# Softmax layers: the order of exponentials, masks, probability splits, bias additions and normalisations on ScalarE and VectorE

## The reference

```
u     = h @ h.T / sqrt(384)                      # per graph, 64 x 64
a     = softmax(u)
delta = a * adjacency
attn  = delta / (sum(delta) + 1e-10)
hl, hs, hr = h @ wl.T + bl,  h @ ws.T + bs,  h @ wr.T + br
ctx   = (attn * upper) @ hl + diag(attn) * hs + (attn * lower) @ hr
o     = (ctx - mean(ctx)) / sqrt(var(ctx) + 1e-12) * g + beta
h     = relu(o)
```

## Time and profile before

| | |
|---|---|
| median of 3 runs | 1877.37 us (1875.14 to 1880.11) |
| the profiled execution | 1874.41 us, its span 1872.6 us |
| TensorE matmul busy | 1732.7 us, 93% of the span |
| VectorE busy | 1254.2 us, 67% |
| ScalarE busy | 886.8 us, 47% |
| GpSimd busy | 817.1 us, 44% |
| largest group | L1092, the values: 637.4 and 399.5 us of matmul time |
| the chain that ended last | TensorE 32% of the span, of it 23% on L1092; VectorE 10%, ScalarE 6% |

### The profile page before, as it was taken

How to read it: one execution, slowest core, us unless ns; L and a number is a source line. 1 busy time by engine, 2 the same in 40 slices (tenths; PEclk the granted TensorE clock), 3 DMA queues, 4 the chain that set the end, 5 groups by cost and what they waited for, 6 DMA issues and landing times.

```text
span 1872.6 us, 30639 instructions
## 1 busy us (share of the span) xinstructions
PE 1732.7 (93%) x9856; PEld 1639.1 (88%) x9856; DVE 1254.2 (67%) x2738; ACT 886.8 (47%) x1783; POOL 817.1 (44%) x848
## 2 busy tenths in 40 slices
PE   7999999999999999995999898999998989989894
PEld 6988888888989888885989898989898989989894
DVE  4586776868585876866567566566575666665656
ACT  4536454554546454554443535444445344343442
POOL 5242432334242432325455356364553564545624
PEclk9999999999999999997999999999999999999997
DMA  6004020301202020302200202002002020020100
GB/s 210 7 23 143 27 85 6 106 6 37 75 22 84 28 84 6 107 16 75 71 1 20 87 0 88 18 20 87 0 30 77 19 87 0 20 87 0 71 1 34
DMA packets 76373, 91.98 MB, mean 49 GB/s; under 512 B 29616, under 2 KB 67504, under 8 KB 76336
## 3 DMA queue, kind: packets, MB, share of 16 engines
q1 hardware_dynamic: 76336, 91.51, 14.8%
HBM read 53.75 MB, written 25.17 MB: 42 GB/s over the span
## 4 chain that ended last, share of the span: by engine, by line
PE 32%; DVE 10%; ACT 6%; issue 5%; DVEq 0%; POOL 0%; ACTq 0%; POOLq 0%
PE s_work L1092 23%; PE s_work L1104 4%; PE b_turn L1053 3%; DVE b_z L1433 2%; DVE b_z L1390 2%; ACT b_z L1191 2%; DVE s_prob_lo L1373 2%; DVE s_fstats L1439 1%; ACT b_z L1199 1%; PE b_score_ps L101 1%; DVE b_turn L1368 1%; ACT s_v_hi L1185 1%; ACT s_expo L1173 1%; DVE s_own L1378 1%; DVE s_v_own L1356 0%
## 5 line engine op out<-in xcount | busy, mean ns | idle before, releaser
L1092 PE MATMUL s_work<-b_w_hi,b_ht 128*128 128x384 f32 x2304 | 637.4, 351 | 0.0
L1092 PEld LDWEIGHTS s_work<-b_w_hi,b_ht 128*128 128x128 f32 x2304 | 440.9, 198 | 0.0
L1092 PE MATMUL s_work<-b_w_lo,b_ht 128*128 128x384 f32 x1152 | 399.5, 347 | 0.0
L359 PE MATMUL g_work<-b_ht,b_w_hi 128*128 128x512 f32 x1152 | 357.5, 391 | 9.8 <-DVE b_w_lo L678 9.8
L1260 POOL TENSOR_TENSOR s_v_lo<-s_v_full,s_v_hi 128x384 fp32r<-128x384 f32 x256 | 242.3, 959 | 266.3 <-ACT s_v_hi L1185 265.8
L612 POOL TENSOR_TENSOR g_qv_lo<-g_v_full,g_qv_hi 128x384 fp32r<-128x384 f32 x128 | 132.7, 1055 | 376.9 <-ACT g_qv_hi L496 376.9
L1356 DVE TENSOR_TENSOR s_v_full<-s_work,b_bias 128x384 f32<-128x384 f32 x256 | 141.1, 556 | 180.2 <-PE s_work L1092 180.2
L359 PEld LDWEIGHTS g_work<-b_ht,b_w_hi 128*128 128x128 f32 x1152 | 215.9, 188 | 52.0 <-issue 9.8
L1092 PEld LDWEIGHTS s_work<-b_w_lo,b_ht 128*128 128x128 f32 x1152 | 228.4, 198 | 0.0
L359 PE MATMUL g_work<-b_ht,b_w_lo 128*128 128x512 f32 x576 | 225.8, 392 | 0.0
L701 DVE TENSOR_TENSOR g_qv_lo<-g_work,g_qv_hi 128x512 fp32r<-128x512 f32 x192 | 128.8, 688 | 117.4 <-ACT g_qv_hi L484 115.6
(11 more groups left out here) (142 smaller groups left out, 3201.9 us busy)
## 6 DMA issues: line engine op xcount, KB each, us to landing
b_x_in<-in_x_t SPq DMA_DIRECT2D x16, 768.0 KB, 7.0
g_x_res<-in_x SPq DMA_DIRECT2D x16, 768.0 KB, 7.6
b_x_in<-x SPq DMA_DIRECT2D x16, 768.0 KB, 5.1
s_x_res<-b_x_in SPq DMA_DIRECT2D x16, 768.0 KB, 5.8
x<-b_z SPq DMA_DIRECT2D x15, 768.0 KB, 3.8
out<-b_z SPq DMA_DIRECT2D x15, 768.0 KB, 3.6
b_a_tr<-in_adj_t SPq DMA_DIRECT2D x64, 64.0 KB, 3.4
g_a_nat<-in_adj SPq DMA_DIRECT2D x32, 64.0 KB, 2.4
```

Source lines behind the costliest of these rows:

```text
L359: mm = pe.matmul(bank[:], w, h, start=(n == 0), stop=(n == len(pairs) - 1))
L1092: mm = pe.matmul(bank[:, 0:H], h, w, start=(n == 0), stop=(n == len(pairs) - 1))
```

## The change

On TensorE the exponentials of layer 1 are turned after value 2 instead of value 3. On ScalarE the probability copies of layer 0 go ahead of the value copies of tile 0 and of normalise; in layer 1 they stay behind both, but ahead of the value copies of tile 1, and normalise goes ahead of the value copies of tile 0. `final_normalise` goes from ahead of the next exponentials to behind normalise of the next unit (steps of unit 3 and, one pass later, unit 0). On VectorE the masks and splits go ahead of all bias additions but number 0 (layer 0) or numbers 0 to 2 or 3 (layer 1), maximum goes ahead of variances, and deviations goes ahead of bias 1 and 2.

```
@@ tensor, one_pass
-                    for j in range(4):
+                    for j in range(SIDES):
                         values(i, unit, j)
                     if layer_of(unit) == 1:
                         turn_exponentials(i, unit)
-                    for j in range(4, 7):
+                    for j in range(SIDES, 7):
                         values(i, unit, j)
@@ scalar
-            def first_half(i, unit):
-                exponentials(i, unit)
-                values_hi(i, unit, 0)
-
-            def second_half(i, unit, more):
+            def rest(i, unit, more):
                 values_hi(i, unit, 1)
-                probabilities_hi(i, unit)
                 if more:
                     turn_out(i, unit + 1, 0)
                     turn_out(i, unit + 1, 1)
...
-            def one_pass(i, last):
+            def one_pass(i, first, last):
 
                 for unit in range(UNITS):
                     more = not (last and unit == UNITS - 1)
                     if more:
-                        first_half(i, unit + 1)
-                    normalise(i, unit, more)
-                    if more:
-                        second_half(i, unit + 1, not (last and unit == UNITS - 2))
-                    if unit >= STREAMS:
-                        final_normalise(i, unit - STREAMS, tiles=NT if more else NT // 2)
+                        exponentials(i, unit + 1)
+                        if layer_of(unit + 1) == 0:
+                            probabilities_hi(i, unit + 1)
+                            values_hi(i, unit + 1, 0)
+                            normalise(i, unit, more)
+                        else:
+                            normalise(i, unit, more)
+                            values_hi(i, unit + 1, 0)
+                            probabilities_hi(i, unit + 1)
+                        if unit == 0 and not first:
+                            final_normalise(i - 1, 1)
+                        if unit == UNITS - 1:
+                            final_normalise(i, 0)
+                        rest(i, unit + 1, not (last and unit == UNITS - 2))
+                        if last and unit == UNITS - 2:
+                            final_normalise(i, 0)
+                    else:
+                        normalise(i, unit, more)
+                        final_normalise(i, 1, tiles=NT // 2)
...
-            first_half(0, 0)
+            exponentials(0, 0)
+            probabilities_hi(0, 0)
+            values_hi(0, 0, 0)
             for n in range(SIDES):
                 weight_hi(n)
-            second_half(0, 0, True)
...
+            rest(0, 0, True)
+            one_pass(0, True, False)
+            with act.Fori(1, PASSES - 1) as i:
+                one_pass(i, False, False)
+            one_pass(PASSES - 1, False, True)
@@ vector, up_to_contexts
-                for j in range(3, 6):
+                if layer_of(unit) == 1:
+                    probabilities(i, unit)
+                    biased_value(i, unit, 3)
+                    probabilities_lo(i, unit)
+                else:
+                    biased_value(i, unit, 3)
+                for j in range(4, 7):
                     biased_value(i, unit, j)
-                probabilities(i, unit)
-                biased_value(i, unit, 6)
-                probabilities_lo(i, unit)
@@ vector, one_pass
-                    variances(i, unit)
                     if not (last and unit == UNITS - 1):
                         if layer_of(unit + 1) == 1:
                             maximum(i, unit + 1)
-                        for j in range(SIDES):
+                            variances(i, unit)
+                            biased_value(i, unit + 1, 0)
+                        else:
+                            variances(i, unit)
+                            probabilities(i, unit + 1)
+                            biased_value(i, unit + 1, 0)
+                            probabilities_lo(i, unit + 1)
+                        deviations(i, unit)
+                        for j in range(1, SIDES):
                             biased_value(i, unit + 1, j)
-                        deviations(i, unit)
                         up_to_contexts(i, unit + 1, last, s if layer == 1 else None)
...
-            for j in range(SIDES):
+            probabilities(0, 0)
+            biased_value(0, 0, 0)
+            probabilities_lo(0, 0)
+            for j in range(1, SIDES):
                 biased_value(0, 0, j)
```

More of the change, by code:

```diff
@@ L1223, in one_pass @@
                     if more:
-                        first_half(i, unit + 1)
-                    normalise(i, unit, more)
-                    if more:
-                        second_half(i, unit + 1, not (last and unit == UNITS - 2))
-                    if unit >= STREAMS:
-                        final_normalise(i, unit - STREAMS, tiles=NT if more else NT // 2)
+                        exponentials(i, unit + 1)
[17 more added lines that the diff above has]
+                        final_normalise(i, 1, tiles=NT // 2)
             act.wait_ge(sh.part_set, 1)
             copy_part(0, 0)
-            first_half(0, 0)
+            exponentials(0, 0)
+            probabilities_hi(0, 0)
+            values_hi(0, 0, 0)
             for n in range(SIDES):
                 weight_hi(n)
-            second_half(0, 0, True)
-            with act.Fori(0, PASSES - 1) as i:
-                one_pass(i, False)
-            one_pass(PASSES - 1, True)
+            rest(0, 0, True)
[3 more added lines that the diff above has]
+            one_pass(PASSES - 1, False, True)
         @block.gpsimd
```

## The result

The changed kernel takes 1791.8 us (median of 4 runs, 1791.7 to 1792.4) against 1877.3 us: a ratio of 0.954, with a 95% interval of 0.953 to 0.956. That is 85.5 us less, where 101.9 were forecast. The profiled execution's span fell from 1872.6 to 1790.6 us, by 82.0. I compare with that number, because the forecast's sum was made against that trace. The time lies inside the stated range (1757 to 1814 us), 16.3 us above the forecast of 1775.5.

A forecast was written before the change was run, and what follows sets the result against it. TensorE's own work plus its first-turn wait for the second probability split, and that wait's clock loss, bound the stretch. Units summed to 815.7 against 915.5 us; with the first unit 101.9 less, 1775.5 us, range 1757 to 1814.

The forecast's parts named there:

- The ceiling and the work of a unit: Softmax stretch: TensorE's bare work is 26.9 us per layer 1 unit, 26.5 per layer 0; at most 116.5 us can go.
- The old wait gone, the clock up: First turn's wait for the second probability split, about 2.2 us plus 1.5 us in clock, goes; clock at 1.0 nearly throughout.
- Rival A: Units 0 and 1: no new wait matters, overlaps in ScalarE's list take up 1.9 us; 1761 us, chance 0.14.
- rival B: Third turn 2 us late in unit 1, 1 us in unit 0, each dragging 1.5 us of clock; 1807 us, chance 0.18.
- rival D: Layer 0: delayed masks and splits starve TensorE of banks at value 5 of units 0 and 1; 1888 us, chance 0.03.
- Units 2 and 3, the bound for the splits: Layer 1: second split at F (fold start) + 11.3 us at latest, ahead of the first turn at F + 11.75; no wait.
- The third turn in unit 1: Later passes: ScalarE's list brings the turned block late, so the third turn waits 1.2 us with overlap.
- I keep this offset: Unit 1 of later passes: VectorE still ends the variances at F (fold start) + 5.0 us, the work ahead being unedited.
- This cover is thin now: Unit 0: GpSimd's last value split ends at F (fold start) + 24.9 us, wanted near F + 25.7; costed at nothing.
- Rival C: GpSimd holds all four residual additions, VectorE 2.7 us late at the masks in units 0 and 1; 1834 us, chance 0.05.

The follow-up runs named there:

- Run 1: The changed kernel with ScalarE's final normalisation again ahead of the next unit's exponentials (layer 0 units of later passes): 1824.0 us.
- Run 5: The changed kernel with TensorE turning the layer 1 exponentials behind value 3 again, one value later: 1791.5 us.
- run 3: The changed kernel with GpSimd's low parts of the values of tiles 2 and 3 computed for only 8 of 384 columns: 1766.1 us.
- run 4: The changed kernel with VectorE's residual additions, final statistics and variance behind bias 2 of the next section, final offset, root and normalisation also moved: 1784.4 us.
- runs 7: The changed kernel with VectorE taking contexts 0 and 1 ahead of the residual additions of tiles 2 and 3 and the final statistics: 1798.2 us.
- 9: The changed kernel with contexts 0 and 1 ahead of the last residual additions, and GpSimd's adjacency masks on 8 columns instead of 512 from pass 1 on: 1783.9 us.
- 10: The kernel of run 4 with bias 3 ahead of the final statistics on VectorE: 1780.9 us.
- run 12: The changed kernel with VectorE's loop over passes written out, without a backward jump: 1791.5 us.

## Why the prediction came out as it did

**The ceiling and the work of a unit: right.** Units 2 and 3 take 26.86 us, unit 1 of the first pass takes 26.44. Subtracting the idle time and 0.17 us of lost overlap from a unit at full clock gave TensorE's work to 0.1 us.

**The old wait gone, the clock up: right.** The largest new wait is 1.1 us, and none lowered the clock. Rival A did not happen, since 5.04 us of new waits stand in each pair of units 0 and 1; nor did rival B, nor rival D: no value of the changed kernel waited for a bank for more than 0.5 us in brackets, 0.7 us by the products. Run 1 shows that the price in D was real, though its place is one value earlier: 2.5 us of delay at the exponentials gave waits of 2.41 and 2.66 us at value 4 and 32 us in all.

**Units 2 and 3, the bound for the splits: right.** Run 5 moved the turned exponentials a value later and changed nothing, so there is at least that much to spare.

**The third turn in unit 1: right.** 1.2 us forecast with the overlap, 0.97 measured. Bias 1, the splits and the turned block all came 0.8 to 1.1 us later than the prediction has them, and TensorE 1.4 us later; the wait kept nearly its size because both lists count from bias 1, as run 3 shows. In unit 0 it was 0.3 forecast and 0.2 measured.

**"I keep this offset": the step that failed.** The prediction kept the variances at F + 5.0 in unit 1, since what is ahead of them hangs on TensorE and is not edited. It is not edited, but its durations changed. The section shrank by 2 to 4 us, the same work of GpSimd now runs without gaps at its end, and the residual additions of VectorE run in the same time: 3.65 and 4.12 us for four, where they took 2.70 before. In unit 0 the 0.95 us more are just what VectorE is late at the contexts (F + 0.35, against 1240.38 = F - 0.59) and at the variances (F + 5.65, against F + 4.7). In unit 1 they are 1.42 us more, of which the later fold hides 0.65, and the variances end at F + 5.8 instead of F + 5.0. Three terms follow from that, in us for units 0 and 1 together: the first value, 1.33 instead of none; value 4, 0.65 instead of none; value 5, 1.23 instead of 0.6 (0.2 and 0.4). The offset itself, taken as 0.2 us, takes 0.60 behind the splits, which is a part of the last: it too has two inputs in SBUF and a low part of GpSimd beside it (1107.18 to 1108.21, the offset 1107.63 to 1108.23), and run 3, which keeps the low parts of tile 0, leaves it at 0.61.

**"This cover is thin now": a warning without a price.** The low parts came late by 0.6 us in unit 0 and, at the end of the kernel, by 1.1 us once. The prediction costed both at nothing. It carried over 1.84 us for each two low parts and had the last one end at F + 24.9; the four took 4.92 us beside the additions, and the last ended at F + 27.3.

Summed, the new waits are 2.37 + 2.67 = 5.04 us for each pair of units, 35.3 us in 7 passes. Forecast were 0.5 + 1.6 = 2.1, 14.7 us. That is 20.6 us short, and with the 1.1 us at the end it covers the 19.9 us between 101.9 and 82.0 (the bare units gave back 15 x 0.04 in layer 1 and 15 x 0.06 in layer 0, 1.5 us together, and 0.3 are the first unit and rounding). By the medians the miss is 16.3 us, since the profiled execution of before lay 3.0 us under its median and that of after 0.6 us above.

**Rival C, in part.** Its mechanism is what happened, its size was not: the additions took 0.98 us on the mean, not 1.38, and the delay of VectorE was 0.8 to 0.95 us, not 2.7, so that no wait grew long enough for the clock. I had put it as a case of its own with a chance of 0.05, all or nothing. It belonged in the sum as a term, with the share of the additions that meet a busy GpSimd.

What shows the cause: run 3 took away only GpSimd work and gave back 25.7 us, with additions at 0.548 us in the median and 0.58 on the mean; run 4 has the same four additions at 4.27 and 2.62 us in one trace by what GpSimd does; runs 7 and 9 show instructions of 4 columns held by GpSimd's masks and freed with them. Run 3 also relieves the contexts directly (0.6 us in unit 0, 4 us in all), and I did not separate the two parts by a run.

The Trainium skill, SBUF — State Buffer, "Who interferes with whom", says that a VectorE instruction with two inputs in SBUF contends with a GpSimd instruction that reads SBUF, and calls the shared pair of ports an exclusive lock. Runs 7 and 9 agree: the held instructions of run 7 end with the mask that was under way, and are short when the masks are.

## What to carry to other kernels

When a change shortens a section, don't keep the offsets of unedited work: list which engine loses its gaps, find the VectorE instructions with two SBUF inputs that will now run beside GpSimd, and put their held durations into the sum. Two lists that wait for each other have to be moved together: VectorE's order alone taken out cost 129 us and the final normalisation alone 32, while the latter put into the old order made it 8 us slower, so the parts don't add. When waits are small, removing one uncovers the next; lay the products of a slow section beside those of an undisturbed one before you price any of them.

## What the runs showed of the hardware

- A hold does not scale with the instruction that is held. VectorE instructions on 4 columns took 1.32 and 1.02 us instead of 0.17 and 0.13 beside GpSimd's masks; the additions of 384 columns took 0.55 free and 1.0 to 1.2 beside GpSimd. One such small instruction is enough to delay a list by over a microsecond.
- VectorE stood idle for 2.4 to 2.7 us at its loop's jump in runs 4 and 10, five times each, with nothing queued and one 8 KB packet on the instruction queue in each idle time. The changed kernel lost nothing at its jump (run 12); it had work under way there and no such packet. Which of the two makes the difference, no run shows.
- GpSimd is slowed as well: its low parts of 384 columns took 4.28 and 4.92 us for four beside the additions, 1.84 for two with no addition beside them.
- The clock: waits of up to 1.70 us (run 4) left it at the upper level. Waits of 2.4 to 2.7 us in run 1 went either way: behind one of 2.66 us it was 0.50 over the next 4 us, behind one of 2.42 us 1.00 (busy times by stretch), and 4 of 14 left it up.

```profile
1145.00:1149.00 4.00, 3.35 (x10) 3.35 (x11) 3.82 (x9) 2.38 (x6) 1.55 (x2) 0.50 0.86 332
...
1232.00:1236.00 4.00, 3.54 (x18) 3.23 (x19) 3.65 (x8) 2.38 (x6) 2.13 (x3) 1.00 0.41 113
```

The waits of about 2 us in the earlier trace rows went either way too.
